# A graph network on one core: VectorE's masking, first pairs and weight splits in another order, and two bias rows added by VectorE instead of TensorE

## The reference

```python
h = relu(layernorm(x));  cond = f(noise)                  # 16 numbers for each node
for i in range(4):                                        # graph transformer, x starts as h
    y = cond_layernorm(x, cond, s1, b1)                   # xn*(1+cond@sw+sb) + cond@bw+bb
    q, k, v = y@wq+bq, y@wk+bk, y@wv+bv                   # 4 heads of 128
    out = softmax over the edges of each source node      # scores q[src]*k[dst], sum of v[dst]
    x = x + out @ wo + bo
    y = cond_layernorm(x, cond, s2, b2)
    x = x + relu(y@m_w1 + m_b1) @ m_w2 + m_b2
x = x_in + x
h = relu(layernorm(x))
out = x + rgcn(relu(rgcn(h)))                             # two relational layers with gates
```

## Time and profile before

| | |
|---|---|
| runs | 2311.95, 2318.28, 2318.28 us, median 2318.28 |
| profiled execution | 2313.26 us, span 2311.5 us, TensorE's mean granted clock .994 |
| busy, share of span | PE 95%, DVE 68%, ACT 49%, POOL 23% |
| chain that ended last | PE 76%, DVE 12%, ACT 5%, issue 5% |
| layer 0's attention passes | 425.7 to about 620 us |
| layer 0's MLP stage | about 622 to 730.8 us |

### The profile page before, as it was taken

The page is one execution under the profiler, slowest core; times in us unless marked ns, Lnnn a source line. Parts: engine busy times, 40 slices in busy tenths (PEclk is TensorE's granted clock), DMA queues, the critical chain, the costliest instruction groups (busy, mean ns, idle before and its releaser), DMA issues.

```text
span 2311.5 us, 36692 instructions
## 1 busy us (share of the span) xinstructions
PE 2195.7 (95%) x13898; PEld 1903.4 (82%) x13898; DVE 1577.9 (68%) x3347; ACT 1121.3 (49%) x1808; POOL 533.8 (23%) x399
## 2 busy tenths in 40 slices
PE   3899979999999999999999999999999999999998
PEld 1565678899888889988888998888899888877877
DVE  9999985588775468877547788754778774343233
ACT  6166643577633357763336775333777533231321
POOL 4000000366400046630005662000665200000000
PEclk9999989999999999999999999999999999999999
DMA  9997781210131020031002103111110421062044
GB/s 250 298 282 243 233 272 35 56 34 23 51 110 31 20 66 23 23 96 68 29 23 63 34 12 109 64 29 31 45 45 1 136 74 29 1 127 37 1 71 106
DMA packets 137379, 189.59 MB, mean 82 GB/s; under 512 B 61285, under 2 KB 61733, under 8 KB 137211
## 3 DMA queue, kind: packets, MB, share of 16 engines
q1 hardware_dynamic: 133208, 180.48, 28.1%
q10 hardware_dynamic: 4003, 6.79, 1.0%
HBM read 155.16 MB, written 32.07 MB: 81 GB/s over the span
## 4 chain that ended last, share of the span: by engine, by line
PE 76%; DVE 12%; ACT 5%; issue 5%; DVEq 1%; DMA 1%; SPq 1%; POOL 0%; ACTq 0%
PE PS L1038 10%; PE PS L1066 9%; PE PS L943 6%; PE PS L945 6%; PE PS L944 6%; PE PS L1052 6%; PE PS L929 5%; PE PS L933 4%; PE PS L930 4%; PE PS L1194 4%; PE PS L1204 4%; PE PS L850 4%; PE PS L801 2%; ACT prob L1435 1%; PE PS L862 1%
## 5 line engine op out<-in xcount | busy, mean ns | idle before, releaser
L782 POOL TENSOR_SCALAR prob<-prob,inv_den 125x1000 f32<-125x1000 f32 x160 | 444.4, 2777 | 0.0
L770 POOL TENSOR_TENSOR rstd<-var_eps,neg_half 125x2 f32<-125x2 f32 x45 | 35.5, 788 | 953.4 <-DVE var_eps L1598 953.4
L1435 ACT ACTIVATE prob<-prob,neg_max 125x1254 f32<-125x1254 f32 x160 | 215.6, 1347 | 56.7 <-DVE neg_max L1950 56.6
L1945 DVE CUSTOM_DVE_ANT_0 prob<-PS,sbias 125x1254 f32<-125x1254 f32 x160 | 233.1, 1457 | 10.0 <-issue 7.3
L1066 PE MATMUL PS<-pT_hi,v_hi 125*128 125x250 f32 x800 | 236.2, 295 | 0.0
L1964 DVE TENSOR_TENSOR pT_lo<-PS,pT_hi 125x1000 fp32r<-125x1000 f32 x160 | 191.1, 1194 | 50.7 <-ACT pT_hi L1452 50.7
L1066 PE MATMUL PS<-pT_lo,v_hi 125*128 125x250 f32 x800 | 224.2, 280 | 0.0
L1066 PE MATMUL PS<-pT_hi,v_lo 125*128 125x250 f32 x800 | 222.6, 278 | 0.0
L1052 PE MATMUL PS<-ident,prob 125*125 125x125 f32 x1600 | 201.1, 273 | 5.6 <-DVE pT_lo L1967 5.5
L1052 PEld LDWEIGHTS PS<-ident,prob 125*125 125x125 f32 x1600 | 195.6, 188 | 12.5 <-issue 7.6
L1450 ACT ACTIVATE pT_hi<-PS 125x1000 fp32r<-125x1000 f32 x160 | 161.9, 1012 | 81.3 <-PE PS L1052 81.3
(11 more groups left out here) (335 smaller groups left out, 5585.6 us busy)
## 6 DMA issues: line engine op xcount, KB each, us to landing
basis_t<-in_L_gnn_basis_dram SPq DMA_DIRECT2D x320, 192.0 KB, 4.9
sbias<-score_bias SPq DMA_DIRECT2D x40, 548.6 KB
adj<-adj SPq DMA_DIRECT2D x20, 546.9 KB
w_lo_raw<-in_L_gnn_m_w_dram SPq DMA_DIRECT2D x8, 1024.0 KB, 6.5
score_bias<-biases SPq DMA_DIRECT2D x10, 548.6 KB
adj<-count SPq DMA_DIRECT2D x10, 546.9 KB
xc<-x_lat SPq DMA_DIRECT2D x12, 448.0 KB
x_first<-x_lat SPq DMA_DIRECT2D x10, 448.0 KB
```

Source lines behind the costliest of these rows:

```text
L782: pool.tensor_scalar(prob[u % 3][:, 0:SPLIT], prob[u % 3][:, 0:SPLIT], inv_den[0:T, u % 4:u % 4 + 1], None, ALU.mult)\
L1435: act.activation(prob[u % 3][:], prob[u % 3][:], ACT.Exp, bias=neg_max[0:T, u % 4:u % 4 + 1], accum_out=den[0:T, u % 4:u % 4 + 1]).then_in ...
L1945: v.tensor_tensor_reduce(prob[u % 3][:].rearrange("p (j s) -> p j s", j=3), PS[0:T, 0:3, 0:SB], sbias[p % 2][a][:].rearrange("p (j s) -> p ...
```

## The change

It has four parts.

- **A, bias rows.** `bo3`, `b23` and their splits are gone, and `rows` is called without a bias row in `out_proj` and `second_layer`. SP loads both rows with `partition_broadcast(128)` into `bo_all` and `b2_all` (256 KB each, before 2 KB each), at the same place of its queue. VectorE adds them to a whole pair of the residual, `add_rows(p, bias)`, ahead of `add_attention(p, 0)` and of `add_mlp(p, 0)`: ten in each layer.
- **B, setup.** Statistics of the second pair move from behind the last score bias to node group 7; the low parts of wq and wv move behind modulations of the second pair; the gates' weights (four tiny operations) move to pair 1 of layer 0. TensorE gets 14 matmuls of 128 columns whose result is not used, between the logarithms of the last group but one and the last.
- **C, first pass.** Of `value_rows(NP-1, 0)` the first two of four chunks (6 matmuls) are made ahead of `scores(0, 0)`, the rest behind it.
- **D, loop order.** `q_low(i+1)` moves from behind `inverse(i, 0)` to behind `masking(i, 1)`; `wo_low(k)` for k = 0, 1, 2 moves into the passes 17 to 19, ahead of `inverse(i, 0)`, and `wo_low(3)` behind the loop.

```diff
@@ constants of the layer
-        bo3, b23 = m("bo3", [128, D], f32r), m("b23", [128, D], f32r)
-        row_raw = m("row_raw", [33, D])
+        bo_all, b2_all = m("bo_all", [128, D]), m("b2_all", [128, D])
@@ SP, after the last scores of a layer
                 wait(sp, s_ps, lay, 8 * NP - 1)
-                sp.dma_start(row_raw[0:1, :], bo[lay:lay + 1, :]).then_inc(rows_in.sem, 16)
-                sp.dma_start(row_raw[32:33, :], m_b2[lay:lay + 1, :]).then_inc(rows_in.sem, 16)
+                sp.dma_start(bo_all[:], bo[lay, :].partition_broadcast(128)).then_inc(rows_in.sem, 16)
+                sp.dma_start(b2_all[:], m_b2[lay, :].partition_broadcast(128)).then_inc(rows_in.sem, 16)
                 load_w(lay, m_w1, w1_raw, 1)
                 load_w(lay, m_w2, w2_raw, 2)
@@ TensorE, setup
+            pe.wait_ge(logs_ready, NT - 1)
+            for k in range(14):
+                pe.matmul(PS[:, 0, 0:128], ones_r[:], ones_r[:], start=True, stop=True)
             pe.wait_ge(logs_ready, NT)
@@ TensorE, attention
                 for i in range(4 * NP):
                     for a in range(2):
+                        if i == a == 0:
+                            qkv_bank_free(pe, v_lo_done, 2 * (NP - 1), lay)
+                            last_value_rows(0, (0, 1), None)
                         scores(i, a)
-                        if i == 0:
+                        if i == 0 and a == 0:
+                            last_value_rows(0, (2, 3), bv3).then_inc(v_ps.sem, 1)
+                        elif i == 0:
                             value_rows(NP - 1, a)
@@ TensorE, out_proj; second_layer likewise
                     rows(mlp_bank(x_added, 2 * p + a), a, oT_hi[p % 2], oT_lo[p % 2], wo_hi, wo_lo,
-                         bo3, lambda k: wait(pe, rows_ready_l, lay, 0) if p == a == 0 and k == 4 else None)\
+                         None)\
                         .then_inc(wo_ps.sem, 1)
@@ VectorE, setup
+                if t == 7:
+                    wait(v, x_loaded[1], "setup", 1)
+                    norm_stats(x_second, "setup", 1)
             score_biases(NT - 1)
-            w_low(wq_hi, wq_lo, wq_raw, "setup", 1)
-            wait(v, x_loaded[1], "setup", 1)
-            norm_stats(x_second, "setup", 1)
-            w_low(wv_hi, wv_lo, wv_raw, "setup", 2)
@@ VectorE, attention
                     for a in range(2):
                         masking(i, a)
+                        if a == 1 and 2 <= i + 1 < 4 * NP:
+                            q_low(i + 1)
                         if i == 0:
                             value_low(NP - 1, a)
                         if i >= 1:
                             pT_low(i - 1, a)
+                        if a == 0 and i > 4 * NP - 4:
+                            wo_low(i - (4 * NP - 4) - 1)
                         inverse(i, a)
-                        if a == 0 and 2 <= i + 1 < 4 * NP:
-                            q_low(i + 1)
-                    if i >= 4 * NP - 4:
-                        k = i - (4 * NP - 4)
-                        wait(v, w_hi_done, lay, k)
-                        v.tensor_tensor(wo_lo[:, k, :], wo_raw[:, k, :], wo_hi[:, k, :].bitcast(fp32),
-                                        ALU.subtract).then_inc(w_lo_done.sem, 1)
+                wo_low(3)
@@ VectorE, MLP stage
                 def add_attention(p, a):
                     if a == 0:
                         wait(v, x_loaded[p], lay, 0 if p < NP - 1 else 1)
+                        add_rows(p, bo_all)
                     wait(v, wo_ps, lay, 2 * p + a)
@@
                 def add_mlp(p, a):
+                    if a == 0:
+                        add_rows(p, b2_all)
                     wait(v, w2_ps, lay, 2 * p + a)
@@
+                def add_rows(p, bias):
+                    link(v.tensor_tensor(x_c[p][:], x_c[p][:], bias[0:T, :].unsqueeze(1).to_broadcast([T, 2, D]), ALU.add))
+
                 wait(v, rows_in, lay, 0)
-                split_row(bo3, row_raw[0:1, :], 0).then_inc(rows_ready_l.sem, 1)
                 add_attention(0, 0)
@@
-                split_row(b23, row_raw[32:33, :], 32).then_inc(rows_ready_l.sem, 1)
                 w_low(w2_hi, w2_lo, w2_raw, lay, W2)
```

More of the change, by code:

```diff
@@ L934, in columns, with rows @@
                 return g
-            def rows(bank, a, x_hi, x_lo, w_hi, w_lo, row3, before=None):
+            def rows(bank, a, x_hi, x_lo, w_hi, w_lo, row3, before=None, chunks=range(4)):
                 o = PS[0:T, bank, :]
                 n = slice(T * a, T * (a + 1))
-                for k in range(4):
+                for k in chunks:
                     if before:
@@ L1856, in bias_row, with gate_weights @@
                 split_row(rb3, rb_raw[l][:], 0).then_inc(r_rows_ready, 1)
-            for l in range(2):
-                gw = cols_all[:, 3, R * 4 * l:R * 4 * (l + 1)].rearrange("p (r c) -> p c r", c=4)
-                link(v.tensor_copy(gw_hl[l][:, :, 0:R], gw))
-                v.tensor_tensor(gw_hl[l][:, :, R:2 * R], gw, gw_hl[l][:, :, 0:R].bitcast(fp32), ALU.subtract)
+            def gate_weights():
+                for l in range(2):
+                    gw = cols_all[:, 3, R * 4 * l:R * 4 * (l + 1)].rearrange("p (r c) -> p c r", c=4)
+                    link(v.tensor_copy(gw_hl[l][:, :, 0:R], gw))
+                    v.tensor_tensor(gw_hl[l][:, :, R:2 * R], gw, gw_hl[l][:, :, 0:R].bitcast(fp32), ALU.subtract)
             for lay in range(LAYERS):
@@ L1901, in _ @@
                     if lay == p == 0:
+                        w_low(wq_hi, wq_lo, wq_raw, "setup", 1)
                         v.wait_ge(adj_stored[1], 32 * 4)
@@ L1909, in _ @@
                         attention_modulate(p + 1, 1)
+                    if lay == p == 0:
+                        w_low(wv_hi, wv_lo, wv_raw, "setup", 2)
                     if p == 0:
@@ L1968, in pT_low, with wo_low @@
                                     pT_hi[i % 2][:, 8:10, n].bitcast(fp32), ALU.subtract).then_inc(pT_lo_done.sem, 1)
+                def wo_low(k):
+                    wait(v, w_hi_done, lay, k)
+                    v.tensor_tensor(wo_lo[:, k, :], wo_raw[:, k, :], wo_hi[:, k, :].bitcast(fp32),
+                                    ALU.subtract).then_inc(w_lo_done.sem, 1)
                 for i in range(4 * NP):
```

10 lines of the change are left out of this document (7 added, 3 removed).

## The result

The changed kernel takes 2287.73 us (median of 4 runs, 2281.82 to 2290.34), the kernel before, run beside it, 2317.93 (4 runs). The ratio is 0.987, 95% interval 0.985 to 0.990: 1.3% faster, 30 us by the medians. The forecast was 2275 with a range of 2260 to 2290. That of the kernel before had a mean granted clock of .994, while 29 further executions of that kernel, run beside the experiments, show .988 to .993 at medians of 2318 to 2319 us.

The account below looks back on a forecast made before the run. The prediction took TensorE, busy 95% of the span, as the bound, its attention gaps waiting for VectorE. Gains of 33 (loop order), 3.0 (setup) and 2.2 (bias rows), 38.2 in all, took 2313.3 to 2275.1 us, range 2260 to 2290.

Parts of the forecast that it names:

- the start: First attention passes of a layer: TensorE's wait of 1.32 filled and q_low moved from ahead of a masking, 1.97 us gained.
- steady passes: Attention loop, 15 passes a layer: earlier masking brings a pass from 9.32 to 9.14 us, 2.9 us gained a layer.
- late passes: Attention passes 17 to 19, five halves of 26.86 us: 3.2 to 3.7 us won a layer, 3.4 taken.
- unexplained slowness of the late halves: Somewhat slower transposes in the late attention halves that wait, cause unknown; leaving it, 23.1 to 23.7 us was to stay.
- the doubt that the sum was above the page's idle time: Attention's 33 us exceeded the 28.5 us idle before the scores; if it erred, it was rather too high.
- q_low's margin: In steady passes q_low was to end only .1 to .3 us before TensorE needs it.
- the rival of the kept pass: Something else keeps the steady pass long, its 2.9 a layer (11.6 in all) not won: 2286.7 us, chance .08.
- The setup: Before the layers: the 2.65 us stall goes and the clock holds; 3.0 us gained, bounds 1.5 and 4.1.
- the rivals on these: Bias rows land late, 2322 us, chance .03; each add takes twice as long, 2305 us, chance .04.
- The walk: Chain of waits through layer 0's MLP stage with the adds: 1.2 us gained, TensorE stalling 1.7 and about 2.3.
- likeliest case: The summed terms hold, 2275.1 us, own range 2268 to 2283: chance .75.
- the hidden adds: Rival: VectorE's chains have unseen slack, so TensorE's shed matmuls count in full: 2257.5 us, chance .10.

Follow-up runs that it names:

- run 5: The changed kernel with 8 and 10 unused matmuls of 512 columns where TensorE stalls for the modulations of pairs 3 and 4: 2277.86 us, ratio 0.983.
- no_warm: The changed kernel without part A and without the 14 unused matmuls of the setup: 2277.8 us, ratio 0.983.
- b2_on_gpsimd: The changed kernel with the 20 adds of the MLP's bias made by GpSimd, the attention's left on VectorE: 2267.56 us, ratio 0.978.
- undo_rows: The changed kernel with part A taken back (bias rows again by TensorE's matmuls and VectorE's row splits), B, C and D kept: 2275.06 us, ratio 0.981.
- b2_on_gpsimd_filled: b2_on_gpsimd with 15 unused matmuls of 128 columns on TensorE ahead of each of the two relational layers: 2263.5 us, ratio 0.976.
- adds_on_gpsimd: The changed kernel with all 40 bias adds made by GpSimd: 2286.33 us.
- part A alone: Only the bias rows change, made on the kernel before: 2324.09 us against 2319.15, ratio 1.0022.

## Why the prediction was right, and where it was not

**Right.** The bound and its reader: TensorE's gaps in attention ended with VectorE's masking. Attention came out at 8.7 to 8.9 a layer for 8.3, the sum nearer than its parts: the start 2.5 and 2.2 (1.97), steady passes 2.3 (2.9; a pass went from 9.33 to 9.18 in the mean of 15, and a half takes 4.58, not 4.57), late passes 4.0 (3.4, the ends of the range were 3.2 and 3.7). The unexplained slowness of the late halves went altogether, down to 4.56 a half; with it the doubt that the sum was above the page's idle time. q_low's margin, the rival of the kept pass, never counted, because the split took .41 and not .73 once it stood elsewhere. The setup gave 4.7 where 1.5 to 4.1 were the bounds: K no longer ran at .50, and the loss of 1.5 ahead of it was .9. The rows landed 4.0 and 6.6 us after their issue at the latest, the adds took 1.22, and the rivals on these are out.

**Right in mechanism, wrong in what follows from it.** The walk put stalls of 1.7 and 2.3 at mods(3,1) and (4,1); the trace has 1.6 to 1.9 and 2.2 to 2.5. It put the stage's gain at 1.2, 1.2, 1.2, −1.4; with the clock held by filler work it is 1.2, 1.05, 1.15, −.7 (run 5). The step that failed is the sum of the walk, "end of stage, 730.78: ... gain 1.2", and the 2.2 made of it: it took TensorE's stalls to cost their length and the work behind them to run at full clock. Measured: −7.9 where the forecast had +2.2; with the clock held it is +2.7, and the clock takes 10.6. The windows of the setup had shown this very thing, a clock of .53 behind the setup's stall of 2.65, and I priced it there and not in the stage where the change made new stalls of nearly that length.

**How near the number was.** The measured 2287.7 lies 12.7 above the forecast of 2275 and outside the likeliest case's own range of 2268 to 2283. It lies within 2260 to 2290, but by luck: halfway to the hidden adds and to the kept pass would have been 2266 and 2281, so the range is wider than its own reason, and its upper end takes in a case, the kept pass at 2286.7, that did not come about. Nothing in it was made for a low clock in the MLP stages. Between the profiled executions attention and setup gave 3.6 more than forecast, the MLP stages 10.1 and the relational layers 5.1 less.

**Not foreseen and not settled.** The relational layers lost 5.1 in the profiled execution: 10.2 us of low clock (6.8 at 1888.5 and 3.4 at 2086.5) behind waits of 1.9 and 1.8 where the kernel before has 1.5 and 1.8. Such stretches sum to 0 in the profiles of before, no_warm and b2_on_gpsimd, 3.4 in undo_rows and b2_on_gpsimd_filled, 6.8 in adds_on_gpsimd and 10.2 in the other five variants and the changed kernel. Where they sum to 0 these layers take 391.7 us, and in the changed kernel 396.8, so the 5.1 are all the clock's. There is no order in it by parts of the change, so part of the 5.1 may be chance of the one execution; the median before lies 4.7 above its profiled execution and that after .9 above its own. The mean granted clocks (.994 in the profiled execution before, .988 to .993 in 29 others of that kernel) say that most runs of before have more time at a low clock than the one that was profiled; where it stands in them wasn't traced.

## What to carry to other kernels

Moving work from the busiest engine to one with idle share in sum gains little if the second stands in chains that the first waits for: 18.6 us shed gave 2.7 with the clock held. And a new stall of TensorE has to be priced twice, by its length and by the low clock that may follow it (1.5 us for each 3.4 here); where it cannot be removed, unused matmuls of the same length in its place gave back 10.6 us here. An operation's own time can change with its place in the queue: the same split took 704 and 410 ns. And before two single profiles are compared, look at the granted clocks of the other runs: by the profiles part A alone costs 10.7 us, by the medians 4.9.
